# Expert results written by plain scatters to one copy per expert rank, instead of scatters that add in memory

## The reference, cut to what matters

```python
def _router(x, gate_w, e_bias):               # 64 experts, 6 per token, chosen within 4 of 8 groups
    ...
    _, idx = jax.lax.top_k(masked, K)         # K = 6
    w = jnp.take_along_axis(scores, idx, axis=1)
    w = w / (w.sum(-1, keepdims=True) + 1e-20) * SCALE
    return (idx, w)
...
pos = jnp.cumsum(oh, axis=0) - oh             # place of a token in its expert's list, over all 2048 tokens
keep = pos < CAP                              # an expert takes 64 tokens, what comes later is dropped
xd = jnp.zeros((E, CAP + 1, D), x.dtype).at[e_flat, slot].set(x[tok])
h = _relu2(jnp.einsum('ecd,eid->eci', xd, w1))
yd = jnp.einsum('eci,edi->ecd', h, w2)
y_assign = yd[e_flat, slot] * gate
routed = jnp.zeros((T, D), x.dtype).at[tok].add(y_assign)
shared = _relu2(x @ shared_up_w.T) @ shared_down_w.T
x = x + (shared + routed)
```

## Time and profile before

| what | value |
|---|---|
| median of three runs | 1375.85 us |
| profiled execution, time | 1376.96 us |
| its span on the core | 1375.1 us |
| busy PE, DVE, ACT, POOL | 84%, 66%, 48%, 43% of the span |
| chain that ended last, by engine | PE 46%, DVE 21%, POOL 11%, issue 9%, ACT 8%, DMA 4% |
| HBM read, written | 104.55 MB, 40.83 MB |

### The profile page before, as it was taken

One profiled execution on the slowest core, in us unless ns is written; L12 is line 12 of the kernel. 1 busy time (PEld: TensorE's weight loads), 2 busy tenths in 40 slices (PEclk: granted clock), 3 DMA queues, 4 the chain that ended last, 5 costly groups with the idle time before them and its releaser, 6 DMA issues.

```text
span 1375.1 us, 24582 instructions
## 1 busy us (share of the span) xinstructions
PE 1148.7 (84%) x8420; PEld 737.2 (54%) x8422; DVE 905.6 (66%) x1846; ACT 658.5 (48%) x1576; POOL 586.5 (43%) x789
## 2 busy tenths in 40 slices
PE   3799997898899978988899978989899978979940
PEld 2355565665555556655555556655455556655520
DVE  4488876565787866656887765656887755661427
ACT  3655423665455514656445325666545235630630
POOL 1255562220377761210577832210777722224760
PEclk9899998999999999998999999999999999989975
DMA  7366542300243304101343322001433535066888
GB/s 311 105 213 198 173 140 73 93 3 20 83 147 108 116 31 115 53 4 33 120 128 106 115 73 70 25 21 33 135 117 100 193 88 145 26 230 227 159 203 309
DMA packets 120139, 159.58 MB, mean 116 GB/s; under 512 B 11632, under 2 KB 82928, under 8 KB 119280
## 3 DMA queue, kind: packets, MB, share of 16 engines
q1 hardware_dynamic: 106384, 131.73, 30.5%
q0 software_dynamic: 9216, 19.98, 5.6%
q10 hardware_dynamic: 4416, 6.29, 1.2%
HBM read 104.55 MB, written 40.83 MB: 106 GB/s over the span
## 4 chain that ended last, share of the span: by engine, by line
PE 46%; DVE 21%; POOL 11%; issue 9%; ACT 8%; DMA 4%; SPq 0%; POOLq 0%; DVEq 0%; ACTq 0%
PE bank L1174 12%; DVE pool_c L1673 5%; PE bank L1216 4%; PE bank L1097 3%; POOL joint L2157 3%; DVE joint L1689 3%; PE bank L1395 3%; PE bank L1354 3%; PE bank L1380 3%; DMA acc<-pool_b,target 2%; POOL xn L2164 2%; PE bank L1479 2%; PE bank L1319 2%; DVE pool_c L1714 2%; PE bank L1195 2%
## 5 line engine op out<-in xcount | busy, mean ns | idle before, releaser
L1174 PE MATMUL bank<-xm,joint 128*128 128x512 f32 x544 | 273.0, 627 | 21.4 <-DVE pool_c L1673 15.6
L2157 POOL TENSOR_TENSOR joint<-joint 128x512 f32<-128x512 f32 x128 | 168.6, 1318 | 248.4 <-DVE joint L1689 247.9
L1673 DVE SCALAR_TENSOR_TENSOR pool_c<-bank,params,pool_c 128x511 f32<-128x511 f32 (+2 forms) x216 | 161.3, 747 | 88.1 <-ACT pool_c L805 82.6
L1174 PEld LDWEIGHTS bank<-xm,joint 128*128 128x128 f32 x544 | 100.3, 198 | 126.2 <-issue 93.9
L1865 DVE TENSOR_REDUCE nmax<-bank 128x1 f32<-128x384 f32 (+3 forms) x176 | 109.6, 637 | 57.4 <-PE bank L1355 56.6
L844 ACT ACTIVATE joint<-bank,dt_ 128x64 f32<-128x64 f32 x512 | 112.1, 343 | 31.6 <-PE bank L1097 31.6
L1216 PE MATMUL bank<-wout,pool_c 128*128 128x256 f32 x512 | 121.8, 381 | 1.2 <-DVE pool_c L1714 1.2
L1216 PEld LDWEIGHTS bank<-wout,pool_c 128*128 128x128 f32 x512 | 95.8, 190 | 33.7 <-issue 22.3
L2151 POOL DMA_INDIRECT xslot<-xrow,slots x96 | 96.9, 1009 | 34.9 <-issue 20.2
L814 ACT ACTIVATE pool_c<-pool_c 128x512 f32<-128x512 f32 x64 | 40.3, 629 | 134.9 <-DVE pool_c L1673 134.9
L1714 DVE TENSOR_TENSOR pool_c<-xn,pool_c 128x512 f32<-128x512 f32 x64 | 89.9, 1405 | 21.6 <-POOL xn L2164 21.6
(11 more groups left out here) (270 smaller groups left out, 2403.2 us busy)
## 6 DMA issues: line engine op xcount, KB each, us to landing
pool_b<-dA_rows SPq DMA_DIRECT2D x64, 256.0 KB, 3.4
pool_b<-dec_rows SPq DMA_DIRECT2D x96, 128.0 KB, 3.6
joint<-pool_b SPq DMA_DIRECT2D x96, 128.0 KB, 2.4
acc<-xrow SPq DMA_DIRECT2D x13, 640.0 KB, 5.8
joint<-dA_rows SPq DMA_DIRECT2D x32, 256.0 KB, 3.2
dA_late<-dA_rows SPq DMA_DIRECT2D x32, 256.0 KB, 4.2
joint<-acc SPq DMA_DIRECT2D x32, 256.0 KB, 7.2
xslot<-xrow SPq DMA_DIRECT2D x16, 321.0 KB, 4.6
```

The source lines that it names most:

```text
L1174: last = mm(bank[:, :], win[:, k, col:col + P], xm[:, k, :], start=(k == 0), stop=(k == KD - 1))
L1673: ins = v.scalar_tensor_tensor(out=cv[:, n:L], in0=bank[:, 0:L - n], scalar=convw[:, ci, TAPS - 1 - n:TAPS - n], in1=cv[:, n:L], op0=ALU.m ...
L2157: M_ready.inc(p.tensor_tensor(M[u % 2][:, hs_, :], Lx[:, hs_, :], cbm[:, c * P:(c + 1) * P].unsqueeze(1).to_broadcast([P, 4, P]), ALU.mult))
```

## The change: what it does

`acc` gets seven copies and a spare row for every place: copy 0 for the residual, copies 1 to 6 for the expert results. An expert that is a token's k-th chosen one (counted by expert number) writes to copy k, so no two scatters write the same row, and the scatters no longer add. VectorE computes the rank with a running sum over each token's 64 selection flags, times the size of a copy, and the router's row grows by 64 words (385 in all) to carry it. A place without a token gets a spare row of its own. `targets` adds token number and copy in two instructions, one for each half of the pair. Waits for the scatter before in a set go; results and row numbers of pair i (from pair 8 on) wait for scatter i - 3. The residual is loaded behind the last token load; the six other copies (48 blocks of 256 KB) are loaded when the last three scatters have landed. VectorE adds five times per block, GpSimd once.

```diff
-XW = D + E + 1
+XW = D + 2 * E + 1
-SETS = 3
-SUMS = 2 * SETS
-FIRST_SET_ENDS = 25
...
+SUMS = 1 + TOPK
...
-        acc = nc.dram_tensor("acc", (SUMS * (NTOK + CAP), D), F32).ap()
+        acc = nc.dram_tensor("acc", (SUMS * (NTOK + CAP) + E * CAP, D), F32).ap()
...
+        wsel, copy_at = xrow[:, :, D:D + E], xrow[:, :, D + E:D + 2 * E]
...
-        def wait_set_before(eng, i):
...
+        def wait_written(eng, i):
+
+            n = len(written)
+            eng.wait_ge(written[i % n].sem, 16 * (i // n + 1))
...
-            wait_set(sp, 0)
+            sp.wait_ge(stored.sem, stored.upto(B))
             for g in range(BLOCKS):
-                load_sums(sp, g, range(2))
-            for s in range(1, SETS):
-                wait_set(sp, s)
+                load_sums(sp, g, range(1))
+            for i in range(PAIRS - len(written), PAIRS):
+                wait_written(sp, i)
             for g in range(BLOCKS):
-                load_sums(sp, g, range(2, 4))
+                load_sums(sp, g, range(1, 4))
...
                 if i >= WB:
-                    wait_added(act, i - WB)
+                    wait_written(act, i - len(written))
...
             for g in range(BLOCKS):
                 load_sums(act, g, range(4, SUMS))
...
                 for t in range(lo, hi):
                     last = v.tensor_scalar(wsel[:, t, :], wsel[:, t, :], r.wrec[:, t:t + 1], SCALE, ALU.mult, ALU.mult)
-                w_ready.inc(last)
+                settle(dve)
+                for t in range(lo, hi):
+                    last = v.tensor_tensor_scan(copy_at[:, t, :], ones[:, 0:E], r.sel[:, t, :], 0.0, ALU.mult, ALU.add)
+                link(last)
+                w_ready.inc(v.tensor_scalar(copy_at[:, lo:hi, :], copy_at[:, lo:hi, :], float(NTOK + CAP), None, ALU.mult))
...
                 if i >= WB:
-                    wait_added(dve, i - WB)
-                target_ready.inc(v.tensor_tensor(target[i % WB][:, :], xd[i % WB][:, XW - 1:XW], sum_at[:, SET_OF[i]:SET_OF[i] + 1], ALU.add))
+                    wait_written(dve, i - len(written))
+                for h in range(2):
+                    rows, col = slice(h * CAP, (h + 1) * CAP), D + E + h * PAIRS + i
+                    last = v.tensor_tensor(target[i % WB][rows, :], xd[i % WB][rows, XW - 1:XW], xd[i % WB][rows, col:col + 1], ALU.add)
+                target_ready.inc(last)
...
-            dve.wait_ge(first_loaded.sem, 16 * 2 * BLOCKS)
-            for g in range(BLOCKS):
-                parts_ = part_sum[g]
-                first_sum.inc(v.tensor_tensor(parts_[0], parts_[0], parts_[1], ALU.add))
+            dve.wait_ge(residual_loaded.sem, 16 * BLOCKS)
             for g in range(BLOCKS):
                 parts_ = part_sum[g]
-                dve.wait_ge(sums_loaded[g].sem, 16 * (SUMS - 2))
-                for q in range(2, SUMS, 2):
+                dve.wait_ge(sums_loaded[g].sem, 16 * TOPK)
+                for q in (1, 3):
                     pair_sum.inc(v.tensor_tensor(parts_[q], parts_[q], parts_[q + 1], ALU.add))
-                dve.wait_ge(first_sum.sem, g + 1)
                 dve.wait_ge(pair_sum.sem, pair_sum.last())
-                pair_sum.inc(v.tensor_tensor(parts_[0], parts_[0], parts_[2], ALU.add))
+                pair_sum.inc(v.tensor_tensor(parts_[0], parts_[0], parts_[1], ALU.add))
                 dve.wait_ge(pair_sum.sem, pair_sum.last())
-                final_sum.inc(v.tensor_tensor(parts_[0], parts_[0], parts_[4], ALU.add))
+                pair_sum.inc(v.tensor_tensor(parts_[0], parts_[0], parts_[3], ALU.add))
+                dve.wait_ge(pair_sum.sem, pair_sum.last())
+                dve.wait_ge(pool_sum.sem, g + 1)
+                final_sum.inc(v.tensor_tensor(parts_[0], parts_[0], parts_[5], ALU.add))
...
-                wait_set_before(pool, i)
                 settle(pool)
-                added[SET_OF[i]].inc(p.indirect_dma_start(acc, bass.IndirectOffsetOnAxis(ap=target[i % WB][:, :], axis=0), ys[i % WB], None,
-                                                      compute_op=ALU.add))
+                written[i % len(written)].inc(p.indirect_dma_start(acc, bass.IndirectOffsetOnAxis(ap=target[i % WB][:, :], axis=0), ys[i % WB], None))
+            for g in range(BLOCKS):
+                pool.wait_ge(sums_loaded[g].sem, 16 * TOPK)
+                pool_sum.inc(p.tensor_tensor(part_sum[g][5], part_sum[g][5], part_sum[g][6], ALU.add))
```

More of the change, by code:

```diff
@@ L63 @@
 ST = SH // P
-XW = D + E + 1
+XW = D + 2 * E + 1
 PAIRS = E // 2
-SETS = 3
-SUMS = 2 * SETS
-FIRST_SET_ENDS = 25
-SET_OF = [i % SETS if i < FIRST_SET_ENDS else 1 + (i - FIRST_SET_ENDS) % (SETS - 1) for i in range(PAIRS)]
-IN_SET = [SET_OF[:i].count(SET_OF[i]) for i in range(PAIRS)]
+SUMS = 1 + TOPK
 BLOCKS = 2 * B
@@ L272, in build @@
         rsums = sb("rsums", [P, AQ])
-        wsel = xrow[:, :, D:D + E]
+        wsel, copy_at = xrow[:, :, D:D + E], xrow[:, :, D + E:D + 2 * E]
         wout_ = wout[:, :, :].rearrange("p c n -> p (c n)")
@@ L307, in build @@
         xd = [carve(pool_b, i * XW, XW) for i in range(WB)]
[L308 to L311, removed]
+        xdT = [carve(pool_b, 3584 + i * 256, 256).rearrange("p (k s) -> p k s", k=KD) for i in range(2)]
+        hr = [carve(pool_b, 4096 + i * P, P) for i in range(2)]
+        hq = [carve(pool_b, 4352 + i * P, P) for i in range(2)]
+        ys = [carve(pool_b, 4608 + i * D, D) for i in range(WB)]
         target = [sb(f"target{i}", [P, 1], U32) for i in range(WB)]
[L314 to L317, removed]
+        WHOLE = BLOCKS * BLOCK_T * D
+        homes = [joint[:, 0:WHOLE], joint[:, WHOLE:2 * WHOLE], pool_a[:, 0:WHOLE], pool_a[:, WHOLE:2 * WHOLE],
+                 pool_c[:, 0:WHOLE], pool_c[:, WHOLE:2 * WHOLE], wout_]
+        part_sum = [[homes[q][:, i * BLOCK_T * D:(i + 1) * BLOCK_T * D] for q in range(SUMS)] for i in range(BLOCKS)]
         w_in_loaded = [signal(f"w_in_loaded{i}", 16) for i in range(2)]
@@ L368, in build @@
             signal(n, start=1) for n in ("xdT_mm", "xdT_ready", "h_mm", "hT_mm", "hr_ready", "hq_ready", "y_mm", "ys_ready", "target_ready"))
-        added = [signal(f"added{i}", 16) for i in range(SETS)]
-        first_loaded = signal("first_loaded", 16)
+        written = [signal(f"written{i}", 16) for i in range(3)]
         sums_loaded = [signal(f"sums_loaded{i}", 16) for i in range(BLOCKS)]
-        first_sum, pair_sum, final_sum = signal("first_sum"), signal("pair_sum"), signal("final_sum")
+        residual_loaded = signal("residual_loaded", 16)
+        pool_sum, pair_sum, final_sum = signal("pool_sum"), signal("pair_sum"), signal("final_sum")
         out_stored = signal("out_stored", 16)
@@ L598, in load_sums @@
                 r0 = q * (NTOK + CAP) + g * BLOCK_T * P
-                (first_loaded if q < 2 else sums_loaded[g]).inc(eng.dma_start(part_sum[g][q], acc[r0:r0 + BLOCK_T * P, :].rearrange("(p t) d -> p (t d)", t=BLOCK_T)))
+                (sums_loaded[g] if q else residual_loaded).inc(eng.dma_start(part_sum[g][q], acc[r0:r0 + BLOCK_T * P, :].rearrange("(p t) d -> p (t d)", t=BLOCK_T)))
         row_loads = [(wq, a["wq"]), (wk, a["wk"]), (wv, a["wv"]), (wo, a["wo"]), (su, a["su"]), (sd, a["sd"])]
@@ L1085, in _ @@
                 ys_ready.inc(ins)
-            for s in range(1, SETS):
-                wait_set(act, s)
+            for i in range(PAIRS - len(written), PAIRS):
+                wait_written(act, i)
             for g in range(BLOCKS):
@@ L2029, in _ @@
             norm(0)
-            v.memset(xrow[:, 0, 0:XW - 1], 0.0)
+            v.memset(xrow[:, 0, 0:D + E], 0.0)
+            v.tensor_scalar(copy_at[:, 0, :], iota64[:, :], float(CAP), float(SUMS * (NTOK + CAP) - NTOK), ALU.mult, ALU.add)
             v.tensor_copy(identb[:, :], ident[:, :])
             v.tensor_copy(xrow[:, 0, XW - 1:XW], small["empty"])
-            for i in range(SETS):
-                v.tensor_scalar(sum_at[:, i:i + 1], sum0[:, 0:1], float(2 * i * (NTOK + CAP)), None, ALU.add)
             for e in range(2):
```

6 lines of the change are left out of this document (removed).

## The result

The changed kernel takes 1386.3 us (median of 4 runs, 1385.09 to 1386.72) against 1376.3 us of the kernel before (4 runs): ratio 1.0069, 95% interval 1.0056 to 1.0082. It is slower, as forecast, but by 10 us instead of 3.5: 6.9 us above the predicted 1379.4. That is 0.3 us above the 1386 at which the range ends; taken against the kernel before, which is 0.5 us slower here than in the runs that the prediction started from, it is just inside (1.0069, where 1386 to 1375.85 is 1.0074). The profiled span is 1384.5 us, 9.4 us longer.

A forecast was written before the change was run, and what follows sets the result against it. It took TensorE to pace the pair loop, then adding scatters' waits and VectorE's additions to bound the end. -17.0 + 15.3 + 4.2 + 0.8 + 0.2 = +3.5 us on 1376.96, 1380.5; as median 1379.4 us, range 1370.5 to 1386.

The forecast's parts named there:

- The end, +15.3: After the last scatter's landing: more copies to read and add, VectorE setting the pace, 45.8 us against 30.5.
- The 1.05 us lost in each block: In the end, GpSimd's addition delays one VectorE addition per block by 1.05 us, making 4.5 us a block.
- The router, +5.0: Rank scans and product on VectorE's path: 4.2 us in three places between rows, 0.8 in the last row.
- Hidden: Rival: the router's added instructions between rows cost nothing; 4.2 us less, 1375.2 us; chance 10%.
- The scatters' waits, -17.0: Pair loop: without adding scatters and their waits the last scatter lands at 1327.6 instead of 1344.6.
- the 2.6 taken: Pair loop: the time in us assumed for a plain scatter to land, from a nearest case of 2.56.
- 0.2 us for the start: Pair loop: the time allowed for the start when working out how long a scatter may take.
- the slack of 4.2 us: Pair loop: the time left for a scatter's issue and landing before the wait for scatter i - 3 delays work.
- the loop falls to the pace of landing: Rival: slow scatter landings set the pair loop's pace; at 5.0 us landing +7 us, 1386.4 us; chance 8%.
- ScalarE and VectorE waiting for scatters in the loop: Sign in the new profile: if ScalarE or VectorE wait for scatters in the pair loop, the forecast is wrong.
- the new loop keeps TensorE's pace: Pair loop: TensorE still sets the pace, 1.79 us a pair, with GpSimd's plain scatters staying below it.
- No cost for the larger clear: First mixer: the clear writes 7.4 MB more, taken as 0, with up to 3 us if loads collide.

The follow-up runs named there:

- e1: The changed kernel with GpSimd's addition moved to VectorE, six additions there per block of the end; 1381.6 us.
- e8: The changed kernel with the rank's scans and product moved, between rows, to where VectorE waits for ScalarE behind best_experts; 1381.7 us.
- e2: The kernel before plus the router's wide rows, scans and product, their result unused, the scatters still adding; 1383.7 us.
- e6: The kernel before with wide rows and the rank's instructions only behind row 0, once, result unused; 1380.4 us.
- e7: The kernel before with wide rows and the rank's instructions three times behind row 0, result unused; 1384.0 us.
- e11: e12 with the rank's instructions between rows moved to where VectorE waits for ScalarE; 1373.2 us, ratio 0.9978 to the kernel before.
- e3: The changed kernel with eight streams of scatters instead of three, so pair i waits for scatter i - 8; 1380.8 us.
- e12: The changed kernel with all six additions on VectorE and eight streams of scatters; 1377.3 us, ratio 1.0015 to the kernel before.
- e10: The kernel before with expert_weights moved, between rows, behind best_experts, the scatters still adding; 1372.4 us.

## Why the prediction was right, and where its sizes were off

The sign came out for the reason given: the end and the router cost more than the loop gained. The size did not: +10 us by the medians for +3.5. Two of the steps below, the clock and the loop, came out dearer than forecast. Both push towards slower, so neither put the sign to a test.

- **The end, +15.3:** measured +14.6. The mechanism (VectorE and GpSimd hold each other up) is shown by e1. The 1.05 us lost in each block were 0.94 to 1.09.
- **The router, +5.0:** it is on the path, as forecast; measured 4.0, since the scans took 0.83 us for four and the product 0.29, less than the 0.92 and 0.4 assumed. "Hidden" is out as it was placed, and e8 shows that another place does hide it.
- **The step that was missing** is the clock: I added up instructions and left the granted clock of the rows that come later as it was, a term put at nothing. It gives 2.96 us at 530 us (e2, e6 and e7 have it, e8 and e11 not) and in sum 2.8. That a shift moves pauses against the clock could not be sized from the kernel before.
- **The scatters' waits, -17.0:** measured -12.2. Landing, alone, was 2.4 us, better than the 2.6 taken. Three things failed. "0.2 us for the start" was 0.8 (results 0 and 1 end at 1278.26 and 1280.06, their scatters start at 1279.15 and 1280.85). The first result stands 9.6 us behind the first token load instead of 8.7. And the slack of 4.2 us was taken from a scatter that always starts in time. One that starts 2.4 us late (the stop at scatter 17), or lands after 5.3 to 5.9 us beside the residual's loads, passes its delay on to every third scatter. That is the rival "the loop falls to the pace of landing", but in the main only from pair 17 on, and it cost 3 to 4 us (71.7 us; 69.0 in e3, 67.9 in e12). By the prediction's own sign, ScalarE and VectorE waiting for scatters in the loop, "the new loop keeps TensorE's pace" was wrong.
- **No cost for the larger clear:** holds in the one trace of each kernel; in the first mixer the shift stays at -0.23 us.

The sum of the forecast was +3.5, measured +9.4 in the profiled span: 1.8 more before the loop, 4.8 in the loop, 0.7 less in the end.

## What to carry to other kernels

Work for a second engine is no relief when the two hold each other up, as VectorE and GpSimd did here with operands in SBUF: price it by the pair, not by the engine. A ring of three waits is only as good as its latest member; with as many waits as there are buffers, eight here, single delays were absorbed. And before a few instructions go onto the path between two phases, look for a place on the same engine where it waits for another: here that was worth more than the instructions' own time (4.1 us for 3), since the clock of later work changed with when that work started.

## What the runs showed that I had not expected

- GpSimd stops before scatter 17 of 32 in every one of the nine kernels with plain scatters, for 3.19 us in six of them and 2.67 to 3.63 in the others, where 0.84 is usual. In the kernels with adding scatters (before, e2, e6, e7, e10) it stands 0.8 to 1.5 us there, where 0.30 is usual. The timeline puts most of these down to the scatter before in the set, but that had landed 2.0 us earlier. The profile shows nothing that it waits for; the cause is open.
- The fall of the clock at 530 us comes or stays away with a shift of 1 us at equal pauses. TensorE's pause of 2.62 us ends at 534.0 in the changed kernel and the clock falls at 534.5; in the kernel before it ends at 533.2, in e8 at 531.7, and the clock stays. Executions also differ in this at 40 to 60 us, where I take the kernels to be alike, by 2.2 to 2.5 us. The Trainium skill, "TensorE: Matmul & The Clock Gate", section Part 1: The HAM clock gate, says that what the gate observes is timed freely and does not start anew with the kernel. By that rule equal pauses can end differently, and these rows agree. But it is not chance that parts the 14 traces here: all nine with the rank's instructions on the path behind row 0 have the fall, the other five do not. In the nine the pause ends 16.0 to 16.8 us after the clock last rose, in the five 14.7 to 15.5 us. That the place of the pause behind that rise is what decides is my reading; no run moves it by itself.
- A plain indirect scatter of 128 rows of 1 KB takes GpSimd 0.96 us, one that adds 1.56.
